# Byte counts, single late root products and a scale chain inside attention in a graph network kernel

## The reference

```python
# layer 0, graph part (dst sums and src sums of the neighbours' rows)
aggr = segment_sum(x[src], dst) / max(count, 1)
h_fwd = aggr @ W_l.T + b_l + x @ W_r.T          # x @ W_r.T is the "root" product
# layer 1, mixing part: linear attention, per head of 64 columns
k, v = instance_norm(k), instance_norm(v)
dots = einsum('nd,ne->de', k, v)
out = (q @ dots / N) @ w_out + b_out
# layer 1, graph part, uses W_l of that layer
```

## Time and profile before

| | us |
|---|---|
| three runs, median (lowest, highest) | 1827.41 (1824.8, 1832.03) |
| the profiled execution | 1833.38 |
| its span, first to last instruction | 1831.6 |
| PE busy in the span | 1674.0 (91%) |
| DVE busy | 966.3 (53%) |
| ACT busy | 669.4 (37%) |
| POOL busy | 235.8 (13%) |
| edge windows, first to last first-chunk product | 50.2 to 433.0 |
| linear attention, first projection to last dots | 1405.8 to 1505.9 |

### The profile page before, as it was taken

The page is one execution under the profiler, slowest core; times in us unless marked ns, Lnnn a source line. Parts: engine busy times, 40 slices in busy tenths (PEclk is TensorE's granted clock), DMA queues, the critical chain, the costliest instruction groups (busy, mean ns, idle before and its releaser), DMA issues. The chain is left out here.

```text
span 1831.6 us, 31389 instructions
## 1 busy us (share of the span) xinstructions
PE 1674.0 (91%) x9423; PEld 1104.4 (60%) x9424; DVE 966.3 (53%) x2821; ACT 669.4 (37%) x1352; POOL 235.8 (13%) x290
## 2 busy tenths in 40 slices
PE   6889888987979899999799899999997989998998
PEld 5344555665747423333656799999955557644657
DVE  7888889887568664244511100000055874345862
ACT  3112444674024576665121344444321432201220
POOL 2100000001010003900044000000065000500002
PEclk8999999999989999999599999999998999999989
DMA  2000121225750000000513312211121002141001
GB/s 85 0 15 29 59 87 67 107 116 194 236 155 7 1 1 1 1 1 1 188 58 115 132 66 90 84 63 66 63 84 34 1 1 82 58 145 42 1 1 60
DMA packets 86409, 118.86 MB, mean 65 GB/s; under 512 B 6789, under 2 KB 72511, under 8 KB 86177
## 3 DMA queue, kind: packets, MB, share of 16 engines
q1 hardware_dynamic: 80992, 106.53, 17.2%
q0 software_dynamic: 3936, 10.37, 1.8%
q10 hardware_dynamic: 1376, 0.66, 0.1%
HBM read 70.66 MB, written 46.87 MB: 64 GB/s over the span
## 5 line engine op out<-in xcount | busy, mean ns | idle before, releaser
L804 PE MATMUL bank<-onehot_key,onehot_low 128*128 128x320 bf16 x1304 | 223.4, 303 | 38.2 <-DVE onehot_low L603 23.8
L599 DVE TENSOR_SCALAR onehot_key<-iota_keys,edge_keys 128x640 bf16<-128x640 f16 x652 | 231.5, 381 | 27.5 <-PE bank L804 22.7
L804 PEld LDWEIGHTS bank<-onehot_key,onehot_low 128*128 128x128 bf16 x1304 | 104.3, 99 | 147.9 <-DVE onehot_key L599 55.0
L2647 ACT ACTIVATE hidden<-bank,b_cols 128x128 f32<-128x128 f32 x344 | 126.4, 367 | 178.2 <-PE bank L2574 154.7
L2728 DVE TENSOR_TENSOR slot_columns<-bank,b_rows 128x256 f32 x43 | 18.3, 425 | 290.3 <-PE bank L2580 290.3
L2574 PEld LDWEIGHTS bank<-slot_columns,w 128*128 128x128 f32 x1376 | 162.8, 194 | 5.6 <-issue 3.4
L2574 PE MATMUL bank<-slot_columns,w 128*128 x1376 | 163.2, 278 | 3.2 <-issue 3.2
L2580 PE MATMUL bank<-w,hidden 128*128 128x256 f32 x688 | 155.6, 379 | 0.0
L671 ACT ACTIVATE edge_low_shifted<-edge_low,window_offset 128x631 f32 x81 | 66.7, 823 | 192.1 <-DVE onehot_low L603 191.2
L2580 PEld LDWEIGHTS bank<-w,hidden 128*128 128x128 f32 x688 | 127.4, 190 | 15.5
L1739 ACT ACTIVATE XT<-bank 128x512 f32<-128x512 f32 x160 | 84.3, 603 | 57.8 <-PE bank L1667 57.8
(11 more groups left out here) (517 smaller groups left out, 2745.4 us busy)
## 6 DMA issues: line engine op xcount, KB each, us to landing
AT_dram<-at_strip SPq DMA_DIRECT2D x20, 640.0 KB, 4.0
A_dram<-a_strips SPq DMA_DIRECT2D x20, 640.0 KB, 2.9
sg_strip<-AT_dram SPq DMA_DIRECT2D x20, 640.0 KB, 4.0
back_strip<-A_dram SPq DMA_DIRECT2D x24, 480.0 KB, 5.0
w<-in_L_ffn_W1p SPq DMA_DIRECT2D x8, 1024.0 KB, 5.3
w<-in_L_ffn_W2p SPq DMA_DIRECT2D x8, 1024.0 KB, 7.8
slot_rows<-ty_zero SPq DMA_DIRECT2D x1, 6144.0 KB, 24.5
slot_columns<-slot_rows SPq DMA_DIRECT2D x12, 512.0 KB, 8.7
```

Of the source, the lines that this page charges most:

```text
L599: dve.tensor_scalar(ohk[:, q, :], ioh[:, :], key[:, ds(chunk(n, offset, q), 1)], None, ALU.is_equal).then_inc(s_key[q], 1)
L804: last = pe.matmul(bank[2 * (x % 2) + h][:, 0:HB], ohl[q // 2][:, :, q % 2], ohk[:, q, h * HB:(h + 1) * HB], start=False, stop=q == Q - 1, ...
L2647: act.activation(hid[:, f, 0:P], bank[f % 4][:, 0:P], ACT.Gelu, bias=b1[:, ds((e + 1) * FB + f, 1)]).then_inc(s_rg, 1)
```

## The change

Four edits:

1. DVE writes one more row in the range chain: `counts`, the number of groups of each window as one byte. In window x=0 PE loads one word of it, four bytes, one for each window of the tile, after its first-chunk products. Each window's upper bound is that word shifted by 8x, masked, and added to the lower bound. PE no longer reads `ranges` but for the first window. DVE and ACT go on as they did.
2. The six late pairs of root products become twelve single tiles. PE makes tile 8 + t behind the last window (x=3) of tile t, for t from 0 to 11, behind turn and forward, and ACT copies it in window x=0 of the next tile, behind its shift and its two copies. The forward products of that window wait for the copy. ACT's straight part is seven tile pairs long.
3. In linear attention the scale chain loses its place at the head. ACT squares after tile 2 and takes the root after tile 7; PE's sum stands behind dots(3); DVE does its parts after tiles 4, 5 and 8.
4. 631 lines are taken out: the tail of the first definition of `experts_stage` and the head of the second, which is the same text as the first's head. The one definition left is word for word the second.

The diff, without the 631 lines and the declaration of the byte type:

```diff
-            FW, RT, CNT = 2 * P + 1, 2, 2 * P
+            FW, CNT = 2 * P + 1, 2 * P
...
-            AHEAD = -(-(ZN - ROOTS) // 2)
+            LATE = T - 2 * ROOTS
+            AHEAD = -(-(LATE + 1) // 2)
...
+                counts = sb(tmp, "group_counts", [1, NW], u8)
...
                         dve.tensor_scalar(rrow[:, 3, 1:NW + 1], rint[:, :], 1.0, None, ALU.max)
+                        dve.tensor_scalar(counts[:, :], rint[:, :], 1.0, None, ALU.max)
...
+                        def late_root_copy(t, k):
+                            act.wait_ge(s_rp, ROOTS + t + 1)
+                            act.activation(XN[:, 2 * ROOTS + t, :], bank[6 + k][:, 0:2 * P], ACT.Copy).then_inc(s_rc, 1)
...
-                            if x == RT + 1 and isinstance(i, int) and ROOTS + i * 2 + k < ZN:
-                                root_copy(ROOTS + i * 2 + k)
+                            if x == 0 and begun and isinstance(i, int) and i * 2 + k - 1 < LATE:
+                                late_root_copy(i * 2 + k - 1, 1 - k)
+                            elif x == 0 and k == 1 and not begun:
+                                late_root_copy(0, 0)
...
-                            following = parts(pe, load_next())
+                            if x == 0:
+                                four = pe.value_load(counts[0:1, w:w + XW].bitcast(i32))
+                            following = pe.compute_val(((four >> (8 * x)) & 255) + before)
...
-                            with pe.Fori(before, following[0]) as n:
+                            with pe.Fori(before, following) as n:
                                 group(n)
...
-                            if x == RT and ROOTS + t < ZN:
+                            if x == XW - 1 and t < LATE:
                                 if t >= 2:
                                     pe.wait_ge(s_fc, t - 1)
-                                roots(ROOTS + t)
+                                late_root(t, k)
...
+                        def late_root(t, k):
+                            for c in range(CB):
+                                tile = 2 * ROOTS + t
+                                last = pe.matmul(bank[6 + k][:, 0:2 * P], XT[:, c, tile * P:(tile + 1) * P], wr[:, c, :], start=c == 0, stop=c == CB - 1)
+                            last.then_inc(s_rp, 1)
...
                             if x == 0:
-                                pe.wait_ge(s_rc, min(ROOTS + t + 1, ZN))
+                                pe.wait_ge(s_rc, ROOTS + min(t + 1, LATE))
                                 pe.wait_ge(s_zm, ZN)
...
                         for t in range(DEEP - 1):
                             kv(t)
-                        pe.wait_ge(s_wq, 1)
-                        for c in range(CB):
-                            last = pe.matmul(bank[7][:, 0:C], onesf[:, :], wsq[:, c, :], start=c == 0, stop=c == CB - 1)
-                        last.then_inc(s_wn, 1)
                         for t in range(T):
                             if t + DEEP - 1 < T:
                                 kv(t + DEEP - 1)
                             dots(t)
+                            if t == 3:
+                                pe.wait_ge(s_wq, 1)
+                                for c in range(CB):
+                                    last = pe.matmul(bank[7][:, 0:C], onesf[:, :], wsq[:, c, :], start=c == 0, stop=c == CB - 1)
+                                last.then_inc(s_wn, 1)
...
                     @block.scalar
                     def _(act):
-                        act.wait_ge(s_sw, 16 * 8)
-                        act.activation(wsq[:, :, :], sg_w[:, :, 0:C], ACT.Square).then_inc(s_wq, 1)
-                        act.activation(gq[:, :, :], sg_gb[:, 0:2, :], ACT.Square).then_inc(s_wq, 1)
-                        act.wait_ge(s_gm, 1)
-                        act.activation(gz[:, 3:6], gz[:, 0:3], ACT.Sqrt).then_inc(s_gr, 1)
...
+                            if t == 2:
+                                act.wait_ge(s_sw, 16 * 8)
+                                act.activation(wsq[:, :, :], sg_w[:, :, 0:C], ACT.Square).then_inc(s_wq, 1)
+                                act.activation(gq[:, :, :], sg_gb[:, 0:2, :], ACT.Square).then_inc(s_wq, 1)
+                            if t == 7:
+                                act.wait_ge(s_gm, 1)
+                                act.activation(gz[:, 3:6], gz[:, 0:3], ACT.Sqrt).then_inc(s_gr, 1)
...
+                            if t == 4:
+                                dve.wait_ge(s_wq, 2)
+                                dve.tensor_reduce(gz[:, 1:2], gq[:, 0, :], AX.X, ALU.max)
+                                dve.tensor_reduce(gz[:, 2:3], gq[:, 1, :], AX.X, ALU.add)
+                            if t == 5:
+                                dve.wait_ge(s_wn, 1)
+                                st.then(dve.tensor_reduce(gz[:, 0:1], bank[7][:, 0:C], AX.X, ALU.max))
+                                dve.tensor_scalar(gz[:, 0:3], gz[:, 0:3], 1e-20, None, ALU.max).then_inc(s_gm, 1)
+                            if t == 8:
+                                dve.wait_ge(s_gr, 1)
```

591 lines of the change are left out of this document (13 added, 578 removed).

## The result

| | before | changed |
|---|---|---|
| median of four runs on one chip | 1826.11 us (1823.38 to 1832.03) | 1800.84 us (1797.51 to 1801.96) |
| profiled execution, its span | 1833.38, 1831.6 | 1801.96, 1800.2 |

The ratio of the changed kernel to the one before is 0.9849, with a 95% interval of 0.9833 to 0.9865: a gain of 25.3 us by these medians and 27.5 by the ratio, where 20.9 were forecast. On two more occasions the ratio was 0.9842 [0.982, 0.9863] and 0.9851 [0.9818, 0.9883], and the medians lay 28.3 and 25.6 us apart.

A forecast was written before the change was run, and what follows sets the result against it. In the edge stage PE and DVE are nearly full and take turns; attention's first dots wait for the scale chain. 10.4 (roots) + 8.6 (load) + 1.9 (attention) = 20.9 us off 1827.4 gives 1806.5; own range 1802 to 1811, wide 1799 to 1819.

The forecast's parts named there:

- the byte load: Edge stage, window x=0: PE's load of one word, not four, is 0.52 us shorter; 0.43 x 20 tiles = 8.6 us.
- attention: Attention's start: first dots 2.8 us earlier, less 0.9 for the squared-weight product now behind tile 3; 1.9 us gained.
- the low stretch behind the first dots: Attention, 1420 to 1424 us, granted clock 0.60: could go with less idle time, worth up to 2.5 us; none counted.
- Roots at x=2: Edge stage, tiles 0 to 5: six uncovered root pairs of 1.74 us vanish from window x=2, 10.4 us gained.
- Roots at x=3: Edge stage: twelve single roots of 0.87 us fall into PE's existing hole at x=0 and cost nearly nothing.
- Costed at nothing: DVE's byte-count operation (about 0.15 us), ACT's twelve single root copies, ACT's longer straight code and the removed lines: 0 us.
- Rival (a): Edge stage: PE's one-word load is no shorter, or a later queue operation replaces it; 12.3 us remain, 1815; chance 0.12.
- Rival (b): Attention: DVE gets in between two POOL additions, first chain not held; item 4.8 us, with clock 7, 1803; chance 0.15.
- Rival (c): Edge stage, window x=0: PE waits for ACT's late root copy, 30 us in all for twelve tiles, 1836; chance 0.04.
- Rival (d): Edge stage: little effect, DVE's own limit returns the 1.74 us or x=3 roots cost 10.4; 1817 to 1820; chance 0.11.

The follow-up runs named there:

- `roots_at_x2`: The changed kernel with the twelve late root products behind window x=2 of their tile in place of x=3: 1807.31 us, ratio 0.9894.
- `attn_only`: The kernel before with only the scale chain's move in attention: 1824.52 us, ratio 0.9972.
- `dve_single`: The changed kernel with POOL's attention additions paced by each tile's keys, and DVE loading one bound per window, not four at x=0: 1805.99 us, ratio 0.9876.
- `before_paced`: The kernel before with POOL's additions to X in attention each waiting for the keys of its tile: median 1826.09 us, ratio 0.9987.

## Why the prediction was right and wrong

Direction and mechanisms held; the size was short by 4 to 8 us. The forecast's own range, 1802 to 1811, missed the median by about 1 us, and the wide range of 1799 to 1819 holds it at its edge. By the ratio and the three runs of the table (0.9849 x 1827.41 = 1799.8) it does so by less than a microsecond.

The step that failed is the size of one term of the sum, the byte load: 8.6 us were put down, and the runs gave 11.6 to 12.0. Two smaller errors stand beside it: attention came out 0.8 us above its term, since the low stretch behind the first dots, left at nothing, became shorter, and the roots 0.3 below theirs. Without the two low stretches of the edge stage the traces give 24.4 us for the change (21.0 in the windows, 0.7 in the first one, 2.7 in attention), 3.5 more than the 20.9 of the sum. What the medians show beyond that, 0.9 to 3.9 us, is of the size by which executions differ.

- **Roots at x=2** (10.4 us): 9.9 to 10.1 measured. DVE's wait of 1.73 was the right row.
- **Roots at x=3** (free): right, by tiles 6 to 11 and by `roots_at_x2`, with one thing missed. I argued that PE's queue loads while PE's array makes the root. That is so: in tiles 2 to 12, but for tile 5, PE's load begins 0.31 to 0.44 us before the first-chunk product, under the root, and without a root 0.20 behind it. What matters as much is that DVE stands still for its own load at that moment.
- **The byte load** (8.6 us, 0.43 a tile): 0.54 a tile in tiles 2 to 19, 1.52 in tile 1 and 0.9 in tile 0, 12 us in all. Three choices were too low. I took PE's 0.49 us for the one word, and it was 0.30; ACT's 0.28, which I gave as the bound, was the nearer row. The load of 0.49 is there again (491 ns) and stands right behind the chain that writes the row, as DVE's single one does (562 ns): that was a row of another situation. I took DVE's limit in one-group tiles from one tile of the earlier trace rows (0.31), and it was among the smallest: in the trace of before DVE waits for PE 0.56, 0.62, 0.41 and 0.57 us in tiles 10 to 13 and 0.40 in tiles 17 to 19, and in tiles 3, 4 and 8 it waits 0.58 to 0.69, above the 0.53 of my upper bound. And I took the median of PE's loads for all: the longest of the earlier trace rows, 1.845 us, is tile 1's. The Trainium skill, "Runtime: NRT & Kernel Launch", section "Instruction fetch mechanics", gives about 200 ns a register, for loads from HBM; the estimate of 12 us from it met the total, but not by its terms. Its 200 ns a register are 300 here for one word and 240 to 250 a word for four, and a load shorter by 0.71 us, more than its 0.6, gave back only 0.54 a tile in tiles 2 to 19.
- **Clock in the edge stage**: not in the sum. I priced the clock in attention alone. The low stretch of 6.8 us in tile 1 was in the trace of before and is worth 1.6 us, the one of 3.4 in the first window 1.7. Both are absent from the changed kernel's first profile, and both are absent from one profile or other of the same edge code as before, so I can't count them as the change's.
- **Attention** (1.9 us): 2.67. The first dots came 2.82 us earlier for 2.8 predicted. L2290 costs its 0.86 us. That leaves 0.7, which goes with the low stretch behind the first dots: 6.8 us in both profiles of before, 3.4 in the changed kernel's first and third and in `attn_only`, and none in its second, where the last dots come 1.7 earlier still. I had left it at nothing.
- **Costed at nothing**: right. The count operation took 0.18 us, and the first window starts at 46.25 us where the second profile of before has 46.28. ACT's waits and copies hold nobody up.
- **Rival (a)** (load no shorter): out, twenty loads of 0.30.
- **Rival (b)** (DVE gets in between additions): didn't happen in three profiles of the changed kernel and in `attn_only`, and did in six profiles of other kernels with the same attention code (two of them with POOL's filling ahead). The rows of before spoke both ways (L2969 and L1175 held, L1017 not), and 0.15 was too small for that. That my forecast of a held L2368 came true in the changed kernel was in part luck. Where it wasn't held, the last dots came 3.3 to 5.3 us earlier than in the changed kernel's first profile, where the rival had 2.9, or 5.1 with its clock.
- **Rival (c)** (PE waits for the root copy): no such wait; ACT waits for PE instead.
- **Rival (d)** (little effect): out, by the table of tiles.

## What to carry to other kernels

Where two engines both pause at the same point of a loop, a third piece of work put there is free on both; find such a point by the engine that runs through, not only by the one that waits. For the price of a register load take the row that stands in the same situation (queue, address, what was written just before), and for a limit take it from every tile. Beside a long unbroken string of additions by POOL, small VectorE operations can take nearly thirty times their length (4.90 us for 0.17), so pace the string by something that happens later. Before a clock effect is booked to a change, look whether another profile of the same code lacks it.

## What the runs showed of the hardware

- One VectorE tensor_scalar of 16 columns beside POOL's string of twenty additions took 0.17 us (string paced), 0.22 to 0.57 (turns taken) or 4.59 to 4.92 (held to the end), with the same operations. Asked at 252 and 256 ns into an addition it was held once and not the other time. What decides is open.
- The Trainium skill, "SBUF — State Buffer", section "SBUF: two separate sides", has the loser wait for one instruction of the other. That describes the turns of 0.65 us; it doesn't describe 4.9 us across seven additions, which three profiles of the changed kernel and `attn_only` show.
- Gaps of 0.1 us between the additions (start to start 0.80 in place of 0.68) were enough for DVE to get in, in the one execution with them: its operations beside the additions took at most 0.72 us.
- A load of one register takes 0.30 us on PE and on DVE and 0.28 on ACT, but fifteen of DVE's 81 in `dve_single` took 0.73 to 0.92, one in each tile from window 17 on. PE's load of four words took 1.00 to 1.02 us in most tiles and 1.84 to 1.87 in tile 1, in all five profiles that have it. Why isn't known.
- The clock's low stretches differ between executions of the same code: after attention it ran 327.1 us in one and 319.7 in another, and tile 1 of the edge stage had 6.8 us at 1.2 GHz in three profiles and none in a fourth. A single profile of a variant, as `before_paced`'s 1817.5 against a median of 1826.1, can show a gain that isn't there.
